# An audio tower on one core: in the last stage, the sixth expert's first layer ahead of the attention scores, the Gelu table behind the shares, a third slot for weighed units, a score bias on end columns only, and the spread's neighbours in another order

## The reference, cut to what matters

```python
h = h + L1_attn(_layernorm(h))       # window K = 7, 16 heads
h = h + L1_ffn(_layernorm(h))        # 6 experts, 341 hidden each
...
    attn = jnp.einsum('bhld,bhlkd->bhlk', q, kg) + bias[None]
    attn = jax.nn.softmax(attn, axis=-1)
    out = jnp.einsum('bhlk,bhlkd->bhld', attn, vg)
    return out @ proj_w.T + proj_b
...
    token_repr = x.mean(axis=1)
    logits = token_repr @ router_w.T
    probs = jax.nn.softmax(logits, axis=-1)
    topk_vals, topk_idx = jax.lax.top_k(probs, TOP_K)
    topk_vals = topk_vals / topk_vals.sum(axis=-1, keepdims=True)
    expert_weights = jnp.einsum('bk,bke->be', topk_vals, pw[topk_idx])
    h = jax.nn.gelu(jnp.einsum('bsd,edf->ebsf', x, W1) + b1[:, None, None, :], approximate=False)
    out_e = jnp.einsum('ebsf,efd->ebsd', h, W2) + b2[:, None, None, :]
    return jnp.einsum('be,ebsd->bsd', expert_weights, out_e)
```

## Time and profile before

| | us |
|---|---|
| median of 3 runs (lowest, highest) | 823.87 (823.41, 824.34) |
| the profiled execution's own time | 823.58 |
| its span | 821.8 |
| of it stage 5 | about 534 to 821.8 |
| turns c = 1 and c = 2 of stage 5 | 32.15, 31.33 |
| turns c = 3 to 6, each (first L2137 to first L2137) | 31.7 |
| busy over the span: PE, DVE, ACT, POOL | 623.6, 632.3, 524.2, 281.4 |

### The profile page before, as it was taken

One profiled execution on the slowest core, in us unless ns is written; L12 is line 12 of the kernel. 1 busy time (PEld: TensorE's weight loads), 2 busy tenths in 40 slices (PEclk: granted clock), 3 DMA queues, 4 the chain that ended last, 5 costly groups with the idle time before them and its releaser, 6 DMA issues.

```text
span 821.8 us, 10987 instructions
## 1 busy us (share of the span) xinstructions
PE 623.6 (76%) x3154; PEld 481.7 (59%) x3155; DVE 632.3 (77%) x1288; ACT 524.2 (64%) x837; POOL 281.4 (34%) x313
## 2 busy tenths in 40 slices
PE   6997651835537182659777999888899999999997
PEld 4564651835537182656455789644666766666665
DVE  1786498999999999999687422257888888887853
ACT  1588999899899999992323334164466565565452
POOL 0464100000000000000178644306456567664542
PEclk9998876858678695969868899999999999999999
DMA  6381042355444445550601566110000000000000
GB/s 182 112 283 60 1 87 37 73 97 106 82 86 77 82 92 99 93 96 1 224 23 47 165 182 186 56 38 0 1 1 10 1 11 10 1 11 10 0 10 19
DMA packets 26385, 56.53 MB, mean 69 GB/s; under 512 B 4203, under 2 KB 15572, under 8 KB 25860
## 3 DMA queue, kind: packets, MB, share of 16 engines
q0 software_dynamic: 5728, 24.56, 15.9%
q1 hardware_dynamic: 19848, 30.80, 12.2%
q10 hardware_dynamic: 764, 0.62, 0.2%
HBM read 29.91 MB, written 10.17 MB: 49 GB/s over the span
## 4 chain that ended last, share of the span: by engine, by line
PE 43%; DVE 25%; issue 13%; ACT 12%; POOL 2%; DMA 2%; SPq 1%; POOLq 1%; DVEq 0%; ACTq 0%
PE psum L2104 5%; PE psum L1812 4%; DVE s_R L1284 4%; DVE s_R L1271 3%; PE psum L2021 3%; PE psum L2029 3%; PE psum L1884 2%; DVE s_R L1295 2%; PE psum L2091 2%; PE psum L1885 2%; PE psum L1886 2%; PE psum L2160 2%; PE psum L2093 2%; PE psum L2092 2%; PE psum L2137 2%
## 5 line engine op out<-in xcount | busy, mean ns | idle before, releaser
L1884 PE MATMUL psum<-s_xn_lo,s_split_hi 128*128 128x368 f32 x256 | 95.1, 371 | 137.2 <-ACT s_R L932 134.9
L1884 PEld LDWEIGHTS psum<-s_xn_lo,s_split_hi 128*128 128x128 f32 x256 | 54.9, 214 | 141.9 <-ACT s_R L932 137.6
L692 POOL DMA_DIRECT2D s_xnfm<-s_R x14 | 17.1, 1219 | 257.5 <-DVE s_R L1295 257.5
L1290 DVE TENSOR_TENSOR_SCAN s_R<-s_R 128x2944 f32<-128x2944 f32 x16 | 100.7, 6292 | 0.8
L1066 ACT ACTIVATE s_R<-psum,s_cols 128x368 f32<-128x368 f32 x96 | 49.5, 566 | 70.0 <-PE psum L2093 70.0
L1885 PE MATMUL psum<-s_xn_hi,s_split_lo 128*128 128x368 f32 x256 | 92.5, 361 | 0.0
L1886 PE MATMUL psum<-s_xn_hi,s_split_hi 128*128 128x368 f32 x256 | 91.8, 359 | 0.0
L2104 PE MATMUL psum<-s_R 128*128 128x368 f32 x256 | 90.1, 478 | 0.0
L788 POOL TENSOR_TENSOR s_R<-s_R 128x368 f32<-128x368 f32 x48 | 46.7, 972 | 62.5 <-DVE s_R L1739 60.8
L751 POOL TENSOR_TENSOR s_R<-s_R 128x368 f32<-128x368 f32 x47 | 54.4, 1157 | 38.0 <-DVE s_R L1609 20.1
L939 ACT ACTIVATE s_R<-psum,s_cols 128x736 f32<-128x736 f32 x64 | 56.0, 876 | 14.5 <-PE psum L1886 10.5
(11 more groups left out here) (263 smaller groups left out, 1598.3 us busy)
## 6 DMA issues: line engine op xcount, KB each, us to landing
s_xnfm<-s_R POOLq DMA_DIRECT2D x14, 1472.0 KB, 10.5
s_R<-in_w SPq DMA_DIRECT2D x28, 256.0 KB, 2.9
s_R<-in_xg SPq DMA_DIRECT2D x7, 744.0 KB, 4.2
x_sorted<-in_x_init SPq DMA_DIRECT2D x1, 5082.0 KB
s_wBC<-in_wBC SPq DMA_DIRECT2D x8, 256.0 KB, 2.6
s_R<-in_v SPq DMA_DIRECT2D x2, 1024.0 KB
s_R<-x_sorted SPq DMA_DIRECT2D x28, 66.0 KB
s_R<-in_w SPq DMA_DIRECT2D x1, 1536.0 KB, 6.5
```

Of the source, the lines that this page charges most:

```text
L1290: dve.tensor_tensor_scan(bufB[:, u], ra[:, u], bufB[:, u], 0.0, ALU.mult, ALU.add).then_inc(ra_free, 1)
L1884: pe.matmul(bank(c), w_hi[:, s, u, k, :], xn_lo[:, a:b], start=True, stop=False)
```

## The change

1. The first layer of e = 5 is moved in front of the scores on PE (entries 18 and 19, right behind the projection), and its Gelus in front of scores_out on ACT. So the hidden tiles of four experts are held. They go to xnfm, where the normalised stream stood in full precision; that copy (L280 for this norm) is gone, and split_stream and stream_sums read bank 5 of PSUM.
2. The Gelu table is loaded behind shares_out, not behind the exponential.
3. ftmp has three slots; a unit waits for the sum of three units ago.
4. weigh_rest is two instructions of two tiles each: the first behind residual_stats, the second behind the second offset. The rest's second layer waits for each half by itself.
5. The score bias of the middle of the window goes in with ACT's scores_out as a bias column; what differs at the ends is added by matmuls over 24 end columns (edges) in place of 368, between the fourth and the fifth product.
6. fill_pause is gone.
7. PE turns the normalised stream before the shares, and does the first half of the rest between the shares and the first spread; router_spread comes two tiles later. DVE splits the stream before it takes the low part of the shares.

```diff
-        fh = take(3, FT, CT)
+        fh = xnfm[:, :].rearrange("p (e j t) -> p e j t", e=4, j=FT)
...
-        ftmp = take(2, CT)
+        ftmp = take(3, CT)
...
-               + [(1, 4, 0), (1, 4, 1)] + [(2, e, j) for e in (2, 3) for j in range(FT)]
-               + [(1, 5, 0), (1, 5, 1)] + [(2, e, j) for e in (4, 5) for j in range(FT)]
+               + [(1, e, j) for e in (4, 5) for j in range(FT)] + [(2, e, j) for e in (2, 3, 4, 5) for j in range(FT)]
...
-                act.activation(S_fm, bank(3, OH), ACT.Copy).then_inc(S_ready, 1)
+                act.activation(S_fm, bank(3, OH), ACT.Identity, bias=col("rpb_mid")[0:OH], scale=1.0).then_inc(S_ready, 1)
...
-                load_table(ACT.Gelu, 1)
...
+                gelus(c - 2, 18, 20)
                 if c < NCH:
                     scores_out(c)
                     exponential(c)
-                gelus(c - 2, 22, 24)
                 if 1 <= c <= NCH:
                     normed_f(c - 1)
+                    norm_copies(act, nF, (c - 1) % 2, c - 1, (5, 5), hi=xn_hi)
                 if c < NCH:
                     shares_out(c)
-                if 1 <= c <= NCH:
-                    norm_copies(act, nF, (c - 1) % 2, c - 1, (5, 5), dst=xnfm, hi=xn_hi)
+                    load_table(ACT.Gelu, 1)
...
-                if g >= 2:
-                    dve.wait_ge(facc_add, added(g - 2))
+                if g >= 3:
+                    dve.wait_ge(facc_add, added(g - 3))
...
-            def weigh_rest(f):
+            def weigh_rest(f, half):
...
-                dve.wait_ge(f_free, 2 + tile_no1(f, NE, NR - 1) + 1)
+                r = slice(half * RH, half * RH + RH)
+                dve.wait_ge(f_free, 2 + tile_no1(f, NE, half * RH + RH - 1) + 1)
...
+                if att:
+                    weigh_rest(f - 1, 0)
                 weigh_expert(f - 1, 2)
...
                 weigh_expert(f - 1, 4)
+                if tail:
+                    split_stream(f)
                 if att:
-                    weigh_rest(f - 1)
                     shares_rest(c)
...
                         if tail:
-                            split_stream(f)
                             stream_sums(f)
+                    if o == 1 and att:
+                        weigh_rest(f - 1, 1)
...
-                for q in range(4):
+                for o in range(K):
+                    q = o % 4
                     m = min(32, OH - 32 * q)
-                    pe.matmul(quarter(q), rpb_w[:, 32 * q:32 * q + m], posc, start=True, stop=False)
-                for o in range(K):
-                    m = min(32, OH - 32 * (o % 4))
                     pe.wait_ge(prod_r, c * K + o + 1)
...
+                    if o == 3:
+                        for q in range(4):
+                            m = min(32, OH - 32 * q)
+                            ins = pe.matmul(edges(quarter(q)), rpb_w[:, 32 * q:32 * q + m], edges(posc),
+                                            start=False, stop=(q + 4 >= K))
...
+                ffn(f - 1, 18, 20)
                 result_tm(c - 3)
                 if att:
                     scores(c)
-                ffn(f - 1, 18, 20)
+                ffn(f - 1, 20, 22)
                 if att:
                     scores_tm(c)
-                ffn(f - 1, 20, 22)
+                ffn(f - 1, 22, 24)
                 if c < 2:
                     keep_busy(8)
-                ffn(f - 1, 22, 26)
+                ffn(f - 1, 24, 28)
+                if tail:
+                    norm_transposes(pe, nF, f % 2, f, (5, 5))
                 if att:
-                    if c >= 2:
-                        fill_pause(1)
                     shares_fm(c)
+                    ffn(f - 1, 28, 30)
...
-                ffn(f - 1, 26, 28)
-                if tail:
-                    norm_transposes(pe, nF, f % 2, f, (5, 5))
...
                     elif o == 6:
+                        ffn(f, 8, 10)
                         if tail:
                             router_spread(f)
-                        ffn(f, 8, 12)
+                        ffn(f, 10, 12)
```

More of the change, by code:

```diff
@@ L278, in norm_copies @@
                     if nm.n == 1 and hi is not None:
-                        act.activation(fm(hi, u), bank(b), ACT.Copy)
-                    ins = act.activation(dst[:, u] if dst is lgx else fm(dst, c), bank(b), ACT.Copy)
+                        ins = act.activation(fm(hi, u), bank(b), ACT.Copy)
+                    else:
+                        ins = act.activation(dst[:, u] if dst is lgx else fm(dst, c), bank(b), ACT.Copy)
                 else:
@@ L525, in audio_tower @@
         NF = len(FFN)
+        RH = NR // 2
         LAST = (7, 6, 5, 3)
@@ L750, in add_expert @@
                     pool.wait_ge(facc_add, added(g - 1))
-                pool.tensor_tensor(facc, ftmp[:, g % 2], ftmp[:, 1 - g % 2] if e == 1 else facc, ALU.add)\
+                pool.tensor_tensor(facc, ftmp[:, g % 3], ftmp[:, (g - 1) % 3] if e == 1 else facc, ALU.add)\
                     .then_inc(facc_add, 1)
@@ L1065, in gelus @@
                         act.wait_ge(f_mm, i + 1)
-                        act.activation(fr[:, j] if e == NE else fh[:, e % 3, j], bank(i % 2), ACT.Gelu,
+                        act.activation(fr[:, j] if e == NE else fh[:, e % 4, j], bank(i % 2), ACT.Gelu,
                                        bias=b1r[:, j:j + 1] if e == NE else col("b1", 2 * e + j), scale=1.0)\
@@ L1074, in rest_out @@
                 act.wait_ge(fo_mm, g + 1)
-                act.wait_ge(facc_add, added(g - 2))
-                act.activation(ftmp[:, g % 2], bank((2, 4)[g % 2]), ACT.Copy).then_inc(fr_out, 1)
+                act.wait_ge(facc_add, added(g - 3))
+                act.activation(ftmp[:, g % 3], bank((2, 4)[g % 2]), ACT.Copy).then_inc(fr_out, 1)
             def qkv_out(c):
@@ L1678, in split_stream @@
                 dve.wait_ge(nF.xT_free, c + 3)
-                dve.tensor_tensor(fm(xn_lo, c % 2), fm(xnfm, c), fm(xn_hi, c % 2).bitcast(f32), ALU.subtract)\
+                dve.tensor_tensor(fm(xn_lo, c % 2), bank(5), fm(xn_hi, c % 2).bitcast(f32), ALU.subtract)\
                     .then_inc(xf_split, 1)
             def stream_sums(c):
-                dve.tensor_reduce(srep, fm(xnfm, c).rearrange("p (b l) -> p b l", b=CB), AX, ALU.add)\
+                dve.tensor_reduce(srep, bank(5).rearrange("p (b l) -> p b l", b=CB), AX, ALU.add)\
                     .then_inc(srep_ready, 1)
@@ L2099, in ffn @@
                                 unit_out(pe, (g - 2) // NU, (g - 2) % NU)
-                            if e == NE:
-                                pe.wait_ge(fr_weighed, f + 1)
-                            else:
+                            if e < NE:
                                 pe.wait_ge(f_free, 2 + tile_no1(f, e, FT - 1) + 1)
-                        ins = pe.matmul(bank((2, 4)[g % 2]), v2[:, n], fr[:, j] if e == NE else fh[:, e % 3, j],
+                        if e == NE and j % RH == 0:
+                            pe.wait_ge(fr_weighed, 2 * f + j // RH + 1)
+                        ins = pe.matmul(bank((2, 4)[g % 2]), v2[:, n], fr[:, j] if e == NE else fh[:, e % 4, j],
                                         start=(j == 0), stop=(j == tiles - 1))
@@ L2128, in result_last @@
                 for j in range(CB):
-                    pe.matmul(psum[0:L, LAST[j], 0:D], ftmp[:, 1, j * L:(j + 1) * L], ident[:, :],
+                    pe.matmul(psum[0:L, LAST[j], 0:D], ftmp[:, (NCH * NU - 1) % 3, j * L:(j + 1) * L], ident[:, :],
                               start=False, stop=True).then_inc(fT_ready, 1)
@@ L2150, in quarter, with edges @@
                 return psum[32 * q:min(32 * q + 32, OH), 3, 0:CT]
+            def edges(x):
+                return bass.AP(x.tensor, x.offset, [list(x.ap[0]), [L, CB], [L - K // 2, 2], [1, K // 2]])
             def scores(c):
                 pe.wait_ge(qkv_ready, c * 3 + 3)
-                for q in range(4):
+                for o in range(K):
+                    q = o % 4
                     m = min(32, OH - 32 * q)
-                    pe.matmul(quarter(q), rpb_w[:, 32 * q:32 * q + m], posc, start=True, stop=False)
-                for o in range(K):
-                    m = min(32, OH - 32 * (o % 4))
                     pe.wait_ge(prod_r, c * K + o + 1)
-                    ins = pe.matmul(quarter(o % 4), sel[:, o, 0:m], prod[:, o], start=False, stop=(o + 4 >= K))
-                    if o + 4 >= K:
+                    ins = pe.matmul(quarter(q), sel[:, o, 0:m], prod[:, o], start=(o < 4), stop=(o >= 4))
+                    if o >= 4:
+                        ins.then_inc(S_mm, 1)
+                    if o == 3:
[3 more added lines that the diff above has]
+                                            start=False, stop=(q + 4 >= K))
                         ins.then_inc(S_mm, 1)
@@ L2168, in scores_tm @@
                 ins.then_inc(ST_ready, 1)
-            def fill_pause(n):
-                for _ in range(n):
```

(5 more changed lines are left out.)

24 lines of the change are left out of this document (13 added, 11 removed).

## The result

The changed kernel takes 813.99 us (812.31 to 815.20), the one before in the same session 823.64 (822.42 to 824.34): ratio 0.9881, 95% interval 0.9867 to 0.9895. A second session gave 815.65 against 823.67, ratio 0.9901 (0.9886 to 0.9916). The forecast was 818.9 with a range from 814.3 to 822.3. It had the right sign and half the gain, 4.7 of 9.65 us. The time lies 0.3 us outside the range in the first session, next to rival A's 814.3, and inside it in the second.

A forecast was written before the change was run, and what follows sets the result against it. PE and DVE, waiting for each other, were taken to bound the kernel. Six turns at -0.62 us (-3.7), c = 1 (-1.3) and the end (+0.3) gave -4.7 from 823.6: 818.9 us, range 814.3 to 822.3.

The forecast's parts named there:

- rival A: All DVE's waits are filled, with no port cost at the router and none at e = 2: 814.3 us, chance 0.18.
- a ring of waits between DVE and PE: In a steady turn DVE and PE wait for each other; filling DVE's 2.70 us of waits shortens the turn unless PE comes later.
- L1558 at the port: With the third slot, DVE's wait of 0.97 us for POOL's sum shrinks by about 0.25, leaving 0.72 at the port.
- the low part's wait: DVE newly waits for the shares' low part behind ACT's copy of the stream: 0.19 us a turn, at most 0.47.
- the port at the router: The rest's second half delays POOL's L788, so small two-operand router instructions run into it: +0.30 us a turn, bounds 0 and 0.9.
- the split: DVE's split, reading PSUM, no longer waits for POOL's add: -0.21 us a turn, no price for PSUM.
- c = 1: This turn weighs no rest; the earlier split and the stream's transposes fill PE's waits: -1.3 us.
- PE therefore comes 1.00 - 0.30 - 0.43 = 0.27 later to e = 2.: Before e = 2, PE gains six matmuls (1.00 us), less 0.30 from the bias and 0.43 of router wait; DVE waits 0.46.
- turns c = 2 and c = 7: First and last of the last stage's six turns, each priced like a steady one at -0.62 us.
- ACT. Cost 0.: ACT's dropped copy, earlier Gelus and later table load cost nothing, as 12.8 us a turn are spare; bounds 0 and 0.15.
- B: The waits only move: router instructions pay 0.9 us at the port, the bias gives PE nothing back; 822.6 us, chance 0.15.
- C: PE's clock falls at new waits around the shares without the filler, 1.3 us in each steady turn: 826.7 us, chance 0.07.

## Why the prediction was wrong

**Right in the steady turn.** The bound (a ring of waits between DVE and PE), the places where the waits would go, and most single terms: L1558 at the port cost 0.83 of the 0.97 (forecast 0.72), the low part's wait is 0.18 (0.19), the first spread's 0.25 (0.31), the port at the router 0.35 (0.30), the split -0.21 (-0.21, and no price for PSUM: 0.53 from PSUM, 0.53 from SBUF), the second fixed part 0.12 (0.08, for which the prediction names no row), and the filler nothing (nothing). The end is +0.25 to +0.45 (+0.3).

**Right in size, in part by luck: c = 1.** It gained 1.2 in the second session (forecast 1.3). But the kernel before had a stretch of low clock there (0.81 over 575 to 580 us), and the second session had none (1.00). With two slots and with the filler back such a stretch is there too, and up to the copy of c = 1 the gain is 0.9 and 1.0. How much of it the waits gave was not tried.

**Wrong: "PE therefore comes 1.00 - 0.30 - 0.43 = 0.27 later to e = 2."** Measured from the router's weights (L1719 and L1722) PE's second layer of e = 2 ends 13.7 us later before and 13.1 in the changed kernel, that is 0.6 sooner, not 0.27 later. Two terms were mis-sized. The two tiles in front of router_spread don't fill a wait of 0.43: they are 1.00 us of work that no longer stands between the router's weights and e = 2, and PE still waited 0.17 for the weights. It had come early, since its waits in front of the shares had shrunk. The bias passes cost 0.18, not 0.5, and gave back 0.57, not 0.30. PE is now 0.6 early. So the wait of 0.46 that I left at e = 2 was not there, and that is the 1.10 - 0.62 = 0.48 a turn. Both are shown one by one: the spread is worth 0.50 on the kernel before and 0.90 in the changed one, the edges 0.45 on the kernel before. The six turns together gained 7.2 where I had 3.7, and 1.9 of the missing 3.5 are this step in the four steady ones.

**Wrong: turns c = 2 and c = 7.** I gave them the steady turn's price. They gained 1.38 and 1.44. Both differ where the port is paid. In c = 2 the four L1558 take 1.74 us, and 1.77 before, so nothing is paid there, and in c = 7 there is no next chunk for them to work on. That accounts for a part at most; why these turns gained more was not tried.

**Right in sum, wrong in its reason: "ACT. Cost 0."** Undoing e = 5's place and the table's costs 3.1 us a turn, of which I estimate 1.3 as clock, and the table's alone 0.95. I found no cost in the move and asked nothing further. It is the condition of the halves: on the kernel before, without it, they make a turn 0.42 slower. My 0.19 for the low part already used ACT's new order without saying that this was what paid for it. Halves without room on ACT is a rival that I did not write down.

**Rivals.** A came true in time in the first session, and in half of its condition (no wait for e = 2, but the port is held). The time is partly luck: A had 9.3 us from stage 5, which gained 7.2 there, and the rest came ahead of the stage. B's port at 0.9 did not happen. C did not happen in the steady turns of the changed kernel, and did in four neighbours of it. The run with the filler back shows that the changed kernel's clock does not need the filler; whether a filler would have held it in those neighbours was not tried.

The steady turns, c = 2 and 7, c = 1 and the end make up the 8.0 us of stage 5 in the second session, within rounding: 4.4 + 2.8 + 1.2 - 0.45. What stays open is why stage 5 began 4.1 us earlier in the first profile. It varies by 5 us with one program, and I tried nothing on it.

## What to carry to other kernels

Where two engines wait for each other in a ring, follow each moved piece from the last hand-over to the next, and count what leaves that path in full; the wait beside it is not its price. Look for what a long instruction hides before you move it: its cover for another engine's lateness has to be paid first, and the move that pays may look free. The same edit can be worth 0.45 us in one order and under 0.1 in most turns of another, so terms are added only along one path.
